# The first FFN token group moved into the last attention group of a gated cross-attention and FFN block

## The chip, the cores and the metric

The kernel runs on one core of a Trainium2 chip. The metric is the time of one execution on the device in microseconds, of which the median of several runs is taken. In the profile, PE is TensorE (PEld its weight loads), DVE is VectorE, ACT is ScalarE, POOL is GpSimd and SP is SyncE, whose queue issues all DMAs here.

## The reference

The input x has 16 sequences of 100 tokens with 512 features; the context has 361 tokens for each sequence. All is float32.

```
x = x + tanh(g_xattn) * attention(layernorm(x), ctx)     # RMS norm with weight, 16 heads of 32, masked softmax,
                                                         # out @ wo.T, times sigmoid(xnorm @ wg.T)
x = x + tanh(g_ffn) * ffn(layernorm(x))
ffn: gate, up = split(x @ w_gu)                          # w_gu: 512 x 2816, 4-bit codes, a scale for each 128 rows
     h = silu(gate) * up                                 # 1408 hidden features
     y = h @ w_down                                      # 1408 x 512, 4-bit codes, a scale for each 128 rows
     y / sqrt(mean(y*y) + 1e-6)
```

Products are made to float32 accuracy from a high and a low part of each operand.

## The kernel before, in words

**Attention.** The 16 sequences are taken in four groups of four (numbers 0 to 3 below). A group has 16 steps, one for each head. In a step PE turns the probabilities of head i (`transpose_probs`), ACT writes the high part of the turned tile (`probsT_hi`) and DVE the low part (`probsT_lo`); PE multiplies head i-1 with the values (`attend`) and DVE divides it (`attn_norm`). DVE takes the row maximum of head i+2 (`row_max`) and ACT its exponential (`exp_step`). Beside this each step has jobs from the hand-written table `BESIDE`: X (turned input), Q and K projections, A and B (values), G (gate product and tanh), T (turned attention output of four heads) and O (output product of one sequence, followed by `output` on DVE, which adds the residual). The steps run in a loop from step 6 to step 5 of the next group. The last group's steps 6 to 15 are written out; after them come `attend` of head 15, T3 and O0 to O3. The jobs of the steps 6 to 10 are G0; Q3, G1; K3; T1, G2; G3. T2 is in step 13. Only G, T and X jobs with a group to serve exist there.

Banks 2 to 5 of PSUM hold the scores of four heads, bank 6 the turned probabilities, bank 7 the attention product, banks 0 and 1 the jobs.

**FFN.** The 1600 tokens are taken in five token groups of 320; a group has 11 hidden tiles of 128 features. For a tile, `products` makes four gate products (one for each 128 input features) and four up products, each a pair of matmuls of 320 columns. The products go round five banks. ACT scales products 0 and 1 of each kind out of PSUM (`scale_product`), DVE adds products 2 and 3 (`scale_add`), POOL adds the two sums (`gate_sum`, `up_sum`), ACT takes tanh, DVE makes `gated` and `times_up`, ACT writes the high part of the hidden tile (`hidden_hi`) and POOL the low part (`hidden_lo`). The down products (`down`) of a group run beside the next group's tiles. The next group's LayerNorm is spread over the tiles: statistics at tiles 0 to 2, `ffn_normalise` at 3 to 5, the turning (`transpose_tile`, `mT_hi`, `mT_lo`) at 5, 7 and 9. The first group's LayerNorm stands in the last attention group, at steps 12 to 15; all its tiles come after the last attention output. Token group 0 holds tokens of attention group 0 only, token group 1 those of attention groups 0 and 1.

**Order.** Every engine runs its own list in order and waits on semaphores. SP's list has the outputs of attention group 2 at steps 2 to 5 of the last group, then the loads of the gate/up weights `wgu` (each behind the job that frees its memory), the group's rows of x1 (`xb`), all down weights `wdn`, the last outputs, and an increment of `s_stored`, for which ACT waits ahead of its first FFN instruction.

Lines of the kernel before that the steps below touch: 226 to 229 (the products' banks, `TURN_AT`), 289 (`STATS_AT`, `TURNED_AT`), 468 and 473 (loads of weights), 483 (load of x1), 671 to 684 (POOL), 880 to 894 (ACT), 1122 to 1148 and 1264 to 1279 (DVE), 1461 (turning), 1574 (products), 1587 (down).

## Time and profile before

| what | value |
|---|---|
| median of 3 runs | 663.53 us (663.25 to 663.76) |
| time of the profiled execution | 666.67 us |
| span of the profiled execution | 664.8 us |
| busy: PE, DVE, ACT, POOL | 589.5, 472.1, 323.3, 223.2 us |
| mean granted TensorE clock | 0.931 of full speed |

A clock of 1.00 in a row is 2.4 GHz, one of 0.50 is 1.2 GHz, and a value between is a stretch with both. Steps 6 to 15 of the last attention group run from 328.4 to about 374 us, the outputs to 390, token group 0 of the FFN from there to 440, and the other four groups to the end.

### The profile page before, as it was taken

Reading aid. Unit: us, or ns where it says so; the run is one execution under the profiler, and the core shown is the slowest. Engines: PE = TensorE matmul, PEld = TensorE weight load, DVE = VectorE, ACT = ScalarE, POOL = GpSimd, SP = SyncE. Lnnn points to the kernel's source line nnn. Section 1 sums busy time; section 2 is a strip of 40 time slices with the busy share of each in tenths; the row PEclk is TensorE's granted clock in tenths of the full one; section 3 lists DMA queues with packets and bytes.
Section 4 is the critical chain, followed back from the end, with each engine's and each line's share of the span. In section 5 each row is a group of like instructions: output and inputs, shape, how many; then the busy total and the mean of one; then the engine's idle time right before and its main releaser. Section 6 shows DMA issues by size and latency. Waiting matters only on the chain.

```text
span 664.8 us, 12492 instructions
## 1 busy us (share of the span) xinstructions
PE 589.5 (89%) x4154; PEld 516.5 (78%) x4154; DVE 472.1 (71%) x1062; ACT 323.3 (49%) x865; POOL 223.2 (34%) x242
## 2 busy tenths in 40 slices
PE   1689998999989899899996776899999998999996
PEld 0678878978779788797885555777798897799984
DVE  6745786867968579686635339989889889877631
ACT  2554454533454334453444115665675665666620
POOL 5630111000120001200000006676686666686640
PEclk9977997989999799878997599899999999999999
DMA  7460033531336222312377330200210020011011
GB/s 263 158 174 3 34 124 100 180 98 50 102 136 188 80 70 70 120 62 104 112 296 272 133 113 0 72 1 0 72 34 5 28 95 10 32 33 33 26 43 43
DMA packets 26841, 59.36 MB, mean 89 GB/s; under 512 B 3624, under 2 KB 3752, under 8 KB 26792
## 3 DMA queue, kind: packets, MB, share of 16 engines
q1 hardware_dynamic: 26792, 58.76, 26.8%
q8 instruction: 24, 0.39, 0.3%
q14 instruction: 25, 0.20, 0.1%
HBM read 39.62 MB, written 19.14 MB: 88 GB/s over the span
## 4 chain that ended last, share of the span: by engine, by line
PE 50%; DVE 23%; issue 10%; ACT 7%; POOL 7%; DMA 2%; DVEq 0%; SPq 0%; ACTq 0%; POOLq 0%
PE bank L257 20%; PE bank L1574 11%; PE bank L1587 10%; PE bank L1422 3%; POOL hT_lo L671 2%; DVE part_gate L1264 2%; PE bank L1398 2%; DVE vb_lo L947 2%; ACT probs L761 2%; DVE pT_lo L984 2%; DVE nmax L979 2%; DVE xn L974 2%; POOL ctxT_lo L603 2%; DVE hidden L1279 1%; POOL part_gate L678 1%
## 5 line engine op out<-in xcount | busy, mean ns | idle before, releaser
L1574 PE MATMUL bank<-mT_hi,wgu 128*128 128x320 f32 x440 | 140.2, 329 | 19.9 <-DVE part_up L1264 8.4
L1574 PE MATMUL bank<-mT_lo,wgu 128*128 128x320 f32 x440 | 133.7, 314 | 0.0
L761 ACT ACTIVATE probs<-bank,nmax 100x96 f32<-100x96 f32 x256 | 66.3, 343 | 128.1 <-DVE nmax L979 128.1
L1574 PEld LDWEIGHTS bank<-mT_hi,wgu 128*128 128x128 f32 x440 | 84.4, 192 | 35.5 <-DVE part_up L1264 12.0
L1574 PEld LDWEIGHTS bank<-mT_lo,wgu 128*128 128x128 f32 x440 | 84.8, 193 | 3.2
L678 POOL TENSOR_TENSOR part_gate<-part_gate 128x320 f32<-128x320 f32 x55 | 57.2, 1040 | 74.2 <-DVE part_gate L1264 74.2
L880 ACT ACTIVATE part_up<-bank,scale 128x320 f32<-128x320 f32 x110 | 57.2, 522 | 50.7 <-PE bank L1574 50.7
L1264 DVE SCALAR_TENSOR_TENSOR part_up<-bank,scale,part_up 128x320 f32<-128x320 f32 x110 | 58.4, 545 | 18.8 <-ACT part_up L880 18.1
L880 ACT ACTIVATE part_gate<-bank,scale 128x320 f32<-128x320 f32 x110 | 52.1, 526 | 35.3 <-SPq L560 19.2
L608 POOL TENSOR_TENSOR rstd<-var,halfpow 100x1 f32<-100x1 f32 x16 | 9.1, 567 | 173.9 <-DVE var L969 173.9
L684 POOL TENSOR_TENSOR part_up<-part_up 128x320 f32<-128x320 f32 x55 | 57.1, 1038 | 25.5 <-DVE part_up L1264 23.5
L1264 DVE SCALAR_TENSOR_TENSOR part_gate<-bank,scale,part_gate 128x320 f32<-128x320 f32 x110 | 55.2, 542 | 13.4 <-ACT part_gate L880 12.7
L1587 PE MATMUL bank<-wdn_lo,hT_hi 128*128 128x512 f32 (+1 forms) x143 | 56.4, 394 | 0.0
L1587 PE MATMUL bank<-wdn_hi,hT_hi 128*128 128x512 f32 (+1 forms) x143 | 56.1, 393 | 0.0
L1587 PE MATMUL bank<-wdn_hi,hT_lo 128*128 128x512 f32 (+1 forms) x143 | 55.8, 390 | 0.0
L1422 PE MATMUL bank<-vb_hi,pT_hi 128*100 128x68 f32 x192 | 51.4, 268 | 0.1
L1422 PE MATMUL bank<-vb_lo,pT_hi 128*100 128x68 f32 x192 | 51.3, 267 | 0.0
L1422 PE MATMUL bank<-vb_hi,pT_lo 128*100 128x68 f32 x192 | 51.3, 267 | 0.0
L671 POOL TENSOR_TENSOR hT_lo<-hidden,hT_hi 128x320 fp32r<-128x320 f32 x55 | 49.4, 898 | 4.6 <-ACT hT_hi L894 3.9
L984 DVE TENSOR_TENSOR pT_lo<-bank,pT_hi 128x300 fp32r<-128x300 f32 x64 | 29.8, 466 | 18.0 <-ACT pT_hi L769 17.3
L979 DVE TENSOR_REDUCE nmax<-bank 100x4 f32<-100x384 f32 x64 | 35.0, 549 | 4.8 <-PE bank L1398 4.8
L947 DVE TENSOR_TENSOR vb_lo<-bank,vb_hi 32x256 fp32r<-32x256 f32 (+2 forms) x56 | 23.6, 422 | 19.3 <-ACT vb_hi L741 14.3
(130 smaller groups left out, 1566.8 us busy)
## 6 DMA issues: line engine op xcount, KB each, us to landing
gate_up_scratch<-left SPq DMA_DIRECT2D x12, 512.0 KB, 6.1
down_scratch<-left SPq DMA_DIRECT2D x12, 512.0 KB, 3.2
wgu<-gate_up_scratch SPq DMA_DIRECT2D x11, 512.0 KB, 7.2
words<-in_packed SPq DMA_DIRECT2D x18, 256.0 KB
xn<-in_x SPq DMA_DIRECT2D x16, 200.0 KB
xa<-in_x SPq DMA_DIRECT2D x16, 200.0 KB
x_scratch<-gate SPq DMA_DIRECT2D x16, 200.0 KB
ctx_raw<-in_ctx_tail SPq DMA_DIRECT2D x4, 768.0 KB, 8.4
```

What stands on the lines that cost most here:

```text
L257: last = nc.tensor.matmul(out_ap, lhs(a, t), rhs(b, t), start=t == 0 and p == 0, stop=t == tiles - 1 and p == 2)
L671: nc.gpsimd.tensor_tensor(hT[LO][:, t, cols], hidden[n % 2][:, :], hT[HI][:, t, cols].bitcast(F32), ALU.subtract)\
L678: nc.gpsimd.tensor_tensor(a[:, :], a[:, :], b[:, :], ALU.add).then_inc(s_gate_sum, 1)
L684: nc.gpsimd.tensor_tensor(a[:, :], a[:, :], b[:, :], ALU.add).then_inc(s_up_sum, 1)
L761: last = nc.scalar.activation(probs[i % 2][:, cols], SC[i % HPG][0:L, cols], ACT.Exp, bias=nmax[:, i % 4, b:b + 1])
L880: nc.scalar.activation(part[n % 2][i][k][:, :], product_bank(j, t, i, k)[:, 0:TG], ACT.Copy, scale=scale32[:, t, i, k:k + 1]).then_inc(s_e ...
L979: nc.vector.tensor_reduce(nmax[:, i % 4, :], SC[i % HPG][0:L, 0:KC].rearrange("t (b k) -> t b k", b=NB), AXIS_X, ALU.max, negate=True).the ...
L984: nc.vector.tensor_tensor(pT[i % 2][LO][:, :, :].rearrange("k c t -> k (c t)"), PT[:, 0:CHUNKS * L], pT[i % 2][HI][:, :, :].rearrange("k c ...
L1264: nc.vector.scalar_tensor_tensor(onto, product_bank(j, t, i, k)[:, 0:TG], scale32[:, t, i, k:k + 1], onto, ALU.mult, ALU.add).then_inc(s_e ...
L1422: last = nc.tensor.matmul(PV[0:L, VW * c:VW * c + 2 * VW].rearrange("t (b w) -> t b w", w=VW), pT[i % 2][ph][:, c, :], vb[vh][:, c, :, VW ...
L1574: last = nc.tensor.matmul(product_bank(j, t, i, k)[:, 0:TG], wgu[t][:, k, 128 * i:128 * i + 128], mT[j % 2][half][:, k, :], start=half == ...
L1587: last = nc.tensor.matmul(bank[6 + slot][0:rows, :], hT[a][:, c, cols], wdn[c][b][:, :], start=c == 0 and p == 0, stop=c == FT - 1 and p == 2)
```

## The change

Token group 0 of the FFN is computed beside the last attention group. Its statistics are taken in step 6, its three row tiles are normalised in steps 7, 8, 9 and turned in steps 8, 9, 10. Its hidden tiles 0 to 4 follow one a step in steps 11 to 15; then come `attend` of head 15 ("H"), tile 5, T3, tile 6, O0, O1, tile 7, O2, O3, and tiles 8 to 10. Token group 1's statistics move to tiles 2 to 4, its normalising to 5 to 7, its turning to 7 to 9. The first two tiles use the product banks 0, 2 and 3, the next six also bank 4, and from then on there are five. Jobs G2 and G3 use bank 0 and O0 to O3 banks 1 and 5 in turn. SBUF is laid out anew so that these tiles find memory; the loads are issued in another order, the down weights with a semaphore for each tile. `ffn_tile` on each engine holds what the loop over tiles held before, in the same order within a tile.

```diff
-        ROUND, TURNED = (5, 2, 0, 3, 4), bank[1]
-        TURN_AT = (5, 7, 9)
+        STATS_AT, NORMED_AT, TURNED_AT = 6, {7: 0, 8: 1, 9: 2}, {8: 0, 9: 1, 10: 2}
+        FIRST_AT = {11: 0, 12: 1, 13: 2, 14: 3, 15: 4}
+        AT_LAST = ("H", 5, "T3", 6, "O0", "O1", 7, "O2", "O3", 8, 9, 10)
+
+        STATS_BESIDE, NORM_BESIDE, TURN_BESIDE = (0, 1, 2), (3, 4, 5), (5, 7, 9)
+        STATS_BESIDE_0, NORM_BESIDE_0, TURN_BESIDE_0 = (2, 3, 4), (5, 6, 7), (7, 8, 9)
+        def turned(j, m):
+            return bank[(6, 7, 1)[m]] if j == 1 else bank[1]
+        def banks_of(n):
+            return (0, 2, 3) if n < 2 else (0, 2, 3, 4) if n < 8 else (0, 2, 3, 4, 5)
+        for n in range(FT * FGROUPS):
+            for p in range(2 * KT):
+                number = min(banks_of(n), key=lambda m: left_at.get(m, (-1, m)))
+                PRODUCT_BANK[n, p], BEFORE[n, p] = number, left_at.get(number)
+                left_at[number] = (n, p)
-        STATS_AT, TURNED_AT = 12, {13: 0, 14: 1, 15: 2}
-        BANK_OF_LAST = {**BANK_OF, **dict(O0=0, O1=1, O2=3, O3=4)}
+        BANK_OF_LAST = {**BANK_OF, **dict(G2=0, G3=0, T2=1, T3=1, O0=1, O1=5, O2=1, O3=5)}
 # SP, in step 13 of the last loop cycle (attention group 2)
+                    elif i == CONTEXT_AT:
+                        sp.wait_ge(s_pj, split_count(GROUPS - 1, "X3"))
+                        for b in range(NB):
+                            sp.wait_ge(s_x1st[b], 32)
+                        load_x1(0)
 # SP, after the last cycle
-                sp.wait_ge(s_ctxlo, KT * GROUPS)
-                sp.wait_ge(s_pj, split_count(GROUPS - 1, "X3"))
-                load_gate_up((5, 6))
                 sp.wait_ge(s_pj, split_count(GROUPS - 1, "B2"))
-                load_gate_up((0, 1, 2, 3, 4))
+                load_gate_up(range(0, 4))
+                sp.wait_ge(s_pj, split_count(GROUPS - 1, "Q3"))
+                load_gate_up(range(4, 5))
                 sp.wait_ge(s_pj, split_count(GROUPS - 1, "K3"))
-                load_gate_up((7, 8, 9, 10))
+                load_gate_up(range(5, FT))
+                load_down(range(0, 1))
+                for b in range(NB):
+                    sp.wait_ge(s_x1st[b], 48)
+                next_x1(1)
                 sp.wait_ge(s_g, NB * GROUPS)
-                for b in range(NB):
-                    sp.wait_ge(s_x1st[b], 32)
-                load_x1(0)
-                load_down()
+                sp.wait_ge(s_sc, STEPS * GROUPS)
+                load_down(range(1, 2))
                 for b in range(NB):
                     output(GROUPS - 1, b, True)
+                    if b == 1:
+                        for other in range(NB):
+                            sp.wait_ge(s_x1st[other], 64)
+                        next_x1(2)
+                load_down(range(2, 10))
                 for b in range(NB):
                     sp.wait_ge(s_x1st[b], 16 * (GROUPS + 1))
-            sp.sem_inc(s_stored, 1)
+                sp.sem_inc(s_stored, 1)
+                load_down(range(10, FT))
 # ACT, DVE and PE, at the end of a step of the last group
+                if last and i in FIRST_AT:
+                    ffn_tile(0, FIRST_AT[i])
 # PE: what a product waits for where no product had its bank before
+                elif PRODUCT_BANK[n, p] == 5:
+                    pe.wait_ge(s_gated, NB * GROUPS)
+                elif beside_attention and PRODUCT_BANK[n, p] == 0:
+                    pe.wait_ge(s_gate, NB * GROUPS)
+                elif beside_attention:
+                    pe.wait_ge(s_exp, STEPS * GROUPS - HPG + PRODUCT_BANK[n, p] - 1)
 # PE, after step 15 (DVE and ACT alike, with their own parts)
-                attend(GROUPS - 1, STEPS - 1)
-                pe.wait_ge(s_mtlo, 3)
-                job(GROUPS, "T3")
-                for b in range(NB):
-                    job(GROUPS, f"O{b}")
+                for part_of in AT_LAST:
+                    if part_of == "H":
+                        attend(GROUPS - 1, STEPS - 1)
+                    elif isinstance(part_of, int):
+                        ffn_tile(0, part_of, True)
+                    else:
+                        job(GROUPS, part_of)
-            for j in range(FGROUPS):
+            for j in range(1, FGROUPS):
                 for t in range(FT):
...
```

POOL's list has the same FFN work as before; it does not name the attention's last steps.

## Rows read from the trace of the kernel before

**Rows 1.** Busy time by stage: stretch, its length, then each engine's busy time.
```profile
core 0: us, PE busy (x) PEld busy (x) DVE busy (x) ACT busy (x) POOL busy (x), PEclk, DMA share, GB/s
328.40:352.40 24.00, 24.00 (x244) 20.45 (x243) 9.32 (x25) 10.35 (x33) 0.00 (x0) 1.00 0.70 259
352.40:374.10 21.70, 12.48 (x85) 11.32 (x84) 13.64 (x43) 7.14 (x22) 0.88 (x1) 0.64 0.84 297
374.10:390.15 16.05, 14.73 (x52) 10.30 (x53) 4.90 (x7) 0.50 (x1) 0.00 (x0) 0.75 0.19 54
390.15:440.20 50.05, 37.76 (x188) 30.59 (x186) 39.80 (x85) 28.57 (x65) 29.10 (x30) 0.90 0.15 45
440.20:640.00 199.80, 192.14 (x1088) 171.16 (x1088) 168.25 (x366) 127.26 (x297) 141.96 (x149) 1.00 0.10 31
```

**Rows 2.** Waits from 395 to 430 us: us in total, times, longest.
```profile
ACT part_gate L880 <- SPq L560: 19.2, 1, 19.2
```

**Rows 3.** The chain of waits: start, duration, what.
```profile
349.44 2.93 PE bank L257 x12
...
368.04 1.11 PE bank L1461 x4
...
376.32 14.01 PE bank L257 x48
...
391.93 2.50 DMA x_scratch<-gate
```

**Rows 4.** Timeline of DVE, steps 11 to 13: start, duration, instruction, idle before it.
```profile
353.35 0.47 DVE L984 TENSOR_TENSOR pT_lo<-bank,pT_hi 128x300 fp32r<-128x300 f32 x1 [3.33 <-ACT pT_hi L769]
...
354.15 0.55 DVE L979 TENSOR_REDUCE nmax<-bank 100x4 f32<-100x384 f32 x1
356.11 0.47 DVE L984 TENSOR_TENSOR pT_lo<-bank,pT_hi 128x300 fp32r<-128x300 f32 x1 [1.42 <-ACT pT_hi L769]
...
357.38 1.86 DVE L1122 BATCH_NORM_STATS2 stats<-xb 128x6 f32<-128x512 f32 x3
...
360.90 1.17 DVE L1140 TENSOR_SCALAR mn<-xb,mv,rstd 128x128 f32<-128x128 f32 x4 [1.00 <-POOL rstd L647]
```

**Rows 5.** Timeline of ACT: one step's exponentials, one scaled product.
```profile
354.73 1.04 ACT L761 ACTIVATE probs<-bank,nmax 100x96 f32<-100x96 f32 x4 [1.42 <-DVE nmax L979]
...
403.01 0.51 ACT L880 ACTIVATE part_up<-bank,scale 128x320 f32<-128x320 f32 x1
```

**Rows 6.** Timeline of DVE: an attention output, then token group 0.
```profile
391.15 0.75 DVE L1005 SCALAR_TENSOR_TENSOR gate<-gate,coef_a,xa 100x512 f32<-100x512 f32 x1
...
401.19 1.00 DVE L1264 SCALAR_TENSOR_TENSOR part_gate<-bank,scale,part_gate 128x320 f32<-128x320 f32 x2
...
404.49 1.00 DVE L1264 SCALAR_TENSOR_TENSOR part_gate<-bank,scale,part_gate 128x320 f32<-128x320 f32 x2
...
410.16 1.07 DVE L1279 TENSOR_TENSOR hidden<-hidden,part_up 128x320 f32<-128x320 f32 x1 [0.75 <-POOL part_up L684]
...
418.84 0.99 DVE L1264 SCALAR_TENSOR_TENSOR part_gate<-bank,scale,part_gate 128x320 f32<-128x320 f32 x2
419.76 0.49 DVE L1279 TENSOR_TENSOR hidden<-hidden,part_up 128x320 f32<-128x320 f32 x1
420.16 2.29 DVE L1140 TENSOR_SCALAR mn<-xb,mv,rstd 64x128 f32<-64x128 f32 x4
...
442.88 1.01 DVE L1264 SCALAR_TENSOR_TENSOR part_gate<-bank,scale,part_gate 128x320 f32<-128x320 f32 x2
```

**Rows 7.** Timeline of PE: one product, a pair of matmuls.
```profile
430.14 0.42 PE L1574 MATMUL bank<-mT_hi,wgu 128*128 128x320 f32 x1 [0.40 <-ACT part_up L880]
430.39 0.31 PE L1574 MATMUL bank<-mT_lo,wgu 128*128 128x320 f32 x1
```

**Rows 8.** SP's queue: first and last of 22 down-weight issues.
```profile
353.41 0.58 SPq L473 DMA_DIRECT2D wdn_hi<-down_scratch  x1
...
364.29 0.43 SPq L473 DMA_DIRECT2D wdn_lo<-down_scratch  x1
```

More of the change, by code:

```diff
@@ L203, in build @@
         s_unit = sem("gate_up_scales_cast")
[L204 removed]
+        s_wgu, s_wdn = [sem(f"gate_up_weight{t}") for t in range(FT)], [sem(f"down_weight{c}") for c in range(FT)]
         s_xb = sem("x1_loaded")
@@ L856, in _ @@
                     mT_hi(0, m)
+                act.wait_ge(s_unit, 1)
+                for t in range(FT):
+                    ffn_tile(0, t)
             with act.Else():
@@ new lines, in ffn_tile @@
+            def ffn_tile(j, t):
+                for n in tiles_done(j, t):
+                    mean_square(n)
+                for k in (2, 3):
+                    scale_add(j, t, 0, k)
+                if t:
+                    times_up(j, t - 1)
+                elif j:
+                    times_up(j - 1, FT - 1)
+                for m in beside_tile(j, t, STATS_BESIDE_0, STATS_BESIDE):
+                    ffn_stats(j + 1, m)
+                for m in beside_tile(j, t, NORM_BESIDE_0, NORM_BESIDE):
+                    ffn_normalise(j + 1, m)
+                for k in (2, 3):
+                    scale_add(j, t, 1, k)
+                gated(j, t)
+                for n in tiles_done(j, t):
+                    output_tile(n)
+                for m in beside_tile(j, t, TURN_BESIDE_0, TURN_BESIDE):
+                    mT_lo(j + 1, m)
@@ L1236, in _ @@
                     mT_lo(0, m)
+                for t in range(FT):
+                    ffn_tile(0, t)
             with dve.Else():
@@ L1319, in _ @@
+            for j in range(1, FGROUPS):
+                for t in range(FT):
+                    ffn_tile(j, t)
             for n in tiles_done(FGROUPS, 0):
@@ L1497, in full_job, with products, down, ffn_tile @@
                 last.then_inc(f_pj, 1)
+            def products(j, t, i, beside_attention):
+                if t == 0 and i == 0:
+                    pe.wait_ge(s_mtlo, 3 * j + 3)
+                if j == 0 and i == 0:
+                    pe.wait_ge(s_wgu[t], 16)
+                for k in range(KT):
+                    open_bank_of(FT * j + t, KT * i + k, beside_attention)
+                    for half in (HI, LO):
+                        last = nc.tensor.matmul(product_bank(j, t, i, k)[:, 0:TG], wgu[t][:, k, 128 * i:128 * i + 128], mT[j % 2][half][:, k, :],
+                                                start=half == HI, stop=half == LO)
+                    last.then_inc(s_gu, 1)
+            def down(n, c):
+                rows, slot = OTILES[n], n % 2
+                cols = ring(128 * n, rows)
+                if c == 0 and n >= 2:
+                    pe.wait_ge(s_yo, n - 1)
+                if n == 0:
+                    pe.wait_ge(s_wdn[c], 32)
+                pe.wait_ge(s_hlo, FT * ((128 * n + rows - 1) // TG) + c + 1)
+                for p, (a, b) in enumerate(PASSES):
+                    last = nc.tensor.matmul(bank[6 + slot][0:rows, :], hT[c][a][:, cols], wdn[c][b][:, :],
+                                            start=c == 0 and p == 0, stop=c == FT - 1 and p == 2)
+                last.then_inc(s_dn, 1)
+            def ffn_tile(j, t, beside_attention=False):
+                for m in beside_tile(j, t, TURN_BESIDE_0, TURN_BESIDE):
+                    if (j, m) == (0, 2):
+                        pe.wait_ge(s_gated, NB * GROUPS)
+                    transpose_tile(j + 1, m)
+                chunks = chunks_beside(j, t)
+                products(j, t, 0, beside_attention)
+                for n, c in chunks[:1]:
+                    down(n, c)
+                products(j, t, 1, beside_attention)
+                for n, c in chunks[1:]:
+                    down(n, c)
             with pe.If(wants_full(pe)):
@@ L1537, in _ @@
                     transpose_tile(0, m)
+                for t in range(FT):
+                    ffn_tile(0, t)
             with pe.Else():
@@ L1578, in down @@
-            def down(n, c):
-                rows, slot = OTILES[n], n % 2
-                cols = ring(128 * n, rows)
-                if c == 0 and n >= 2:
-                    pe.wait_ge(s_yo, n - 1)
-                if n == 0 and c == 0:
-                    pe.wait_ge(s_wdn, 16 * 2 * FT)
-                pe.wait_ge(s_hlo, FT * ((128 * n + rows - 1) // TG) + c + 1)
-                for p, (a, b) in enumerate(PASSES):
-                    last = nc.tensor.matmul(bank[6 + slot][0:rows, :], hT[a][:, c, cols], wdn[c][b][:, :],
-                                            start=c == 0 and p == 0, stop=c == FT - 1 and p == 2)
-                last.then_inc(s_dn, 1)
@@ L1603, in _ @@
+            for j in range(1, FGROUPS):
+                for t in range(FT):
+                    ffn_tile(j, t)
             for n in TILES_BESIDE[FGROUPS]:
```

400 lines of the change are left out of this document (204 added, 196 removed).

## The prediction

> **What bounds the kernel now.** I read four views: the busy time by stage, the waits, the chain of waits, and the timeline of each engine where the change works.
>
> By stage [rows 1], PE is busy for all 24.00 us of the steps 6 to 10 at a clock of 1.00, while DVE has 9.32 and ACT 10.35 us of work: PE sets that stage, and the chain runs through its jobs (349.44, a job of 12 matmuls of 512 columns, 2.93 us) [rows 3]. From 352.4 on nobody is full. In the steps 11 to 15 PE has 12.48 us of 21.70, at a clock of 0.64; from 374 to 390 the four output products hold PE, with DVE at 4.90 of 16.05; and token group 0 of the FFN lasts 50.05 us with PE at 37.76, DVE at 39.80, ACT at 28.57 and POOL at 29.10. These are 88 us in which each engine has work for 42 to 65. Token group 0's hidden tiles depend on x rows that were finished three attention groups earlier, so the two idle stages can be laid over each other. In the four groups behind 440.2 PE is at 192.14 of 199.80 us; the change does not touch their work.
>
> I measure by two DVE instructions that both kernels have. `pT_lo` of step 11 starts at 353.35 [rows 4]; the first `scale_add` of group 1's tile 0 starts at 442.88 [rows 6]. Between them lie 89.5 us.
>
> **Steps 6 to 10: +1.5 us.** Statistics (1.86 us) and their POOL power, then three normalisings (1.17 us each while POOL is idle) [rows 4], go into steps 6, 7, 8 and 9. With three `mT_lo` (about 0.6, by the 300-column 0.47 of `pT_lo`) that is about 7.5 us more on a DVE that idles 14.7 us there [rows 1], so most is hidden. PE is the full engine: its three turnings took 1.11 us for four transposes at a clock of 0.50 [rows 1, 3]; at 1.00 I take half, and for the third (64 rows) a quarter, 1.3 us together. Step 8's normalising and `mT_lo` also stand ahead of `pT_lo` of step 9, so that the maximum and exponential of head 11 are 1.7 us late, but the scores that need their bank come only behind T1, G2 and a turning on PE, which covers all but 0.2 us. Bounds: 1.1 (turnings alone) and 4 (the 2.9 us of one job's cover gone as well). The load of x1 now sits in step 13 of the loop cycle before; its waits are for things long done. ACT's new wait for the kept weight pieces is met by the time it comes.
>
> **Steps 11 to 15: 28.5 us where there were 21.** Each step now has a tile behind its attention work on every engine. For tiles 0 and 1 there are three banks, so product 3 waits for ACT's first scaling, and ACT comes to it only behind the exponential. Link by link from the start of one `pT_lo` to the next: `pT_lo` 0.39 and `attn_norm` 0.41 (starts 353.35 to 354.15), maximum 0.55, exponentials 0.05 + 1.04, scaling of product 0 0.53, hand-over and product 3 0.10 + 0.56 (430.14 to the end of the pair at 430.70), `scale_add` 0.54, POOL's gate sum 0.26 + 1.05, tanh 0.5, `gated` 0.5, together 6.35 [rows 4, 5, 6, 7] (POOL: 29.10 us in 30, and the full sums are slightly longer than that mean [rows 1]). The same stretch took 2.76 us before (353.35 to 356.11). Step 13 has four banks, but T2 and a statistic as well: 6.7. In steps 14 and 15 maximum and exponential are gone and DVE's own work sets the pace: attention 0.8, scaled sums 2 x 0.93, `times_up` 0.4, `gated` 0.4, a statistic 0.6 = 4.05, and with aggregation, variance and the last division 5.05. Sum 6.35 + 6.35 + 6.7 + 4.05 + 5.05 = 28.5. Nothing hides these links. Bounds: 5 x 4.05 = 20 if no link waits, and 5 x 8 = 40 if tanh and products of each tile are paid in full behind exponentials.
>
> **Tiles 5 to 10 with the outputs: 34.2 us.** In group 0 before, plain tiles came every 3.30 us (401.19 to 404.49) [rows 6], which is POOL's three operations; a tile with a normalising took 4.8, because the normalising beside POOL takes 2.29 us and not 1.17 (418.84: sums, `times_up` 0.40, 2.29) [rows 4, 6]. Now: tile 5 4.8; T3 0.5; tile 6 4.8; O0 and O1 3.9; tile 7 with normalising and `mT_lo` 5.6; O2 and O3 3.7; tile 8 3.9; tile 9 3.7; tile 10 3.3. The output figures: two jobs cost PE 5.6 to 5.9 us [rows 3], DVE 2 x 1.47 (0.72 + 0.75) [rows 6]; PE finishes tile 6's products 1.2 us into DVE's tile, so the jobs run under the rest of it and DVE waits about 1 us. Total 34.2 by DVE. PE for itself needs 6 x 2.35 for products and some 14 for outputs, transposes and turnings, 28 us at 1.00, so it is not the bound.
>
> **What goes away** within the 89.5: ACT's first FFN instruction waited 19.2 us for `s_stored` behind the last stores (2.50 us of DMA in the chain) [rows 2, 3]. Now ACT meets that wait ahead of group 1. SP has 16 weight issues ahead of it; 22 took 11.4 us [rows 8], so 16 take 8.2, and tiles 8 to 10 (10.9 us) cover them with some 2 us to spare. The same 4 MB of `wdn` at the 297 GB/s of the second stage [rows 1] land in 14 us, and group 1 asks for two a tile from 12 us on: just hidden. The loads of `wgu` begin behind the same output of attention group 2 as before, in step 5, and the first tile asks for its weights in step 11, 24 us and more later [rows 1].
>
> **Clock: +4 us.** With about 3.6 us of matmuls (at 1.00) in a step of 6.3, PE is 56% busy. The rows have 0.64 for a stage with about a third of its time in full-clock work, and 0.90 for group 0 [rows 1]. I take half the time at 1.2 GHz in steps 11 to 15, where each such step costs 1.1 us more (transposes, and two or three products on the chain, 0.15 a matmul), 2.5 us; and 1.5 in the outputs (48 matmuls took 14.01 us at 0.75 against 4 x 2.93) [rows 1, 3]. Bounds 0 and 11. The Trainium skill ("TensorE: Matmul & The Clock Gate", What's actually happening) has it that the throttled state is the default and activity releases it. The trace agrees, 0.64 in the thin stage and 1.00 behind 440 us. By that rule alone the filled steps would run at 1.00 and the 4 us would be 0.
>
> **POOL beside attention outputs: +1 us.** DVE's `times_up`, with both inputs in SBUF, took 1.07 us beside POOL at 410.16 and 0.49 at 419.76 [rows 6]. The four residual additions (L1005, 0.75) had an idle POOL and now have a busy one. Bounds 0 and 4 x 1.05. The Trainium skill ("SBUF — State Buffer", Who interferes with whom) says that a DVE instruction with two SBUF inputs waits out a GpSimd instruction that reads SBUF, as one lock. Row 410.16 agrees; each addition held for a whole POOL instruction would give the upper bound.
>
> **Sum.** 1.5 + 28.5 + 34.2 + 4 + 1 = 69.2 us in place of 89.5: -20.3. The profiled execution of 666.67 us becomes 646.4. The median of the runs, 663.53, is 3.1 us below it; with the same difference it becomes **643.2 us**.
>
> **The rivals.**
>
> *Longer steps (B).* Handshakes between four in-order lists seldom meet as well as on paper. For it: DVE waited 3.33 us for ACT at 353.35 and 1.42 at 356.11 with hardly any other work [rows 4]. Against: most of 6.35 us is already waits. At 8 us a step in place of 5.7, +11.5: 654.7.
>
> *Outputs and tiles at 1.2 GHz (C).* For it: PE's clock was 0.64 and 0.75 in the two stages before 390 [rows 1]. Products 25.6, outputs 4 x 5.6 = 22.4, rest 4 and waits 2, 54 in place of 34.2 + 1.5: +18, 661. Against: PE is over 80% filled there at full clock.
>
> *The second half of SP's list (D).* `s_stored` or `wdn` come late, at 220 GB/s or with slower issues: ACT or `down` waits 2 to 6 us at group 1's start: 647. For it: only 2 us of margin.
>
> *All meets well (E).* Clock 1.00 and four-bank steps at 5: 643.2 - 4 - 3.5 = 636.
>
> *Slower than before (F).* A step of 11 to 15 pays the attention's round (2.76 us) and a tile's whole passage, product to `up_sum`, one behind the other. The passage alone is 7 us: product 0.6, scaling and sums 1.6, POOL's gate and up sum 2.6, tanh, `gated` and `times_up` 1.5, hand-overs 0.7 [rows 5 to 7]; with a statistic and a division 10.7 us a step, 53.5 for five: +25 on the forecast's 28.5, 668. It decides from 5.7 + 20.3 / 5 = 9.8 us a step. Against it: in group 0 successive tiles overlapped down to 3.30 us.
>
> *It does not do what it says (G).* If a wait on a late bank or load kept tiles 0 to 4 out of the steps, they would follow them: about as before, 662. The waits of products are for `s_exp`, `s_gate` and `s_gated`, each done by the time that the tile's turn comes, so this is unlikely.
>
> **How the numbers follow.** Forecast (637 to 649) 0.55, B 0.18, C 0.05, D 0.09, E 0.07, F 0.03, G 0.03. The range leaves out E's better half, and C, F and G: 636 to 655. Faster by over 0.2% (1.3 us, about what a measurement tells from none): all but F and part of G, 0.95; within 0.2% 0.02, slower 0.03.
>
> **What would show it.** Right: DVE from `pT_lo` of step 11 to group 1's first `scale_add` in about 69 us; step 11 starts 1 to 2 us later; `pT_lo` starts 6 to 7 us apart in steps 11 to 13 and 4 to 5 behind them; ACT's wait for `s_stored` gone or under 1 us; the stretch behind it as long as before (222 us). Wrong: steps of 8 us or more (B, F), a clock under 0.8 in the output stage (C), a wait of PE for a DMA or of ACT for SP at group 1's first tile (D), more than 3 us gained or lost behind it.

## The result, and the profile after

The changed kernel takes 647.24 us in the median of 4 runs (640.88 to 651.23), beside 663.64 us for the kernel before; the ratio is 0.9711, 95% interval 0.9632 to 0.9791. Forecast were 643.2 us and 636 to 655. The profiled execution is the 651.23 us one, the longest of the four and left out of the ratio; its span is 649.4 us beside 664.8. Where its extra time sits turned out to be the main finding, so it is kept as the trace of after.

I cut both traces at four instructions that both kernels have, all on DVE: `pT_lo` of the first step of the first group, `pT_lo` of steps 6 and 11 of the last group, and the first `scale_add` of FFN group 1.

| stretch, us | before | after | difference | forecast |
|---|---|---|---|---|
| start to first `pT_lo` | 47.13 | 53.00 | +5.87 | 0 |
| to step 6 of the last group | 282.48 | 282.34 | -0.14 | 0 |
| steps 6 to 10 | 23.74 | 25.24 | +1.50 | +1.5 |
| step 11 to group 1's first `scale_add` | 89.53 | 65.93 | -23.60 | -21.8 |
| from there to the end | 221.92 | 222.89 | +0.97 | 0 |

So steps 6 to 10 and the rebuilt stretch together give 22.1 us, 1.8 more than forecast, and the profiled execution gets 15.4 of them. Of the rest, 5.9 us go at the start, in code whose work the change does not touch, and 1.0 behind group 1's first `scale_add`.

By stage, after: steps 6 to 10, steps 11 to 15, tiles 5 to 10 with the outputs, in the columns of [rows 1].
```profile
335.34:360.58 25.24, 25.01 (x252) 21.15 (x244) 15.11 (x47) 11.56 (x35) 0.88 (x1) 1.00 0.74 270
360.58:390.34 29.76, 25.09 (x154) 21.99 (x154) 22.30 (x59) 18.69 (x48) 13.37 (x14) 0.89 0.11 34
390.34:426.51 36.17, 32.66 (x161) 26.36 (x160) 31.30 (x62) 17.17 (x40) 17.81 (x20) 0.91 0.45 148
```
The two thin stages of before (PE 12.48 of 21.70 and DVE 4.90 of 16.05) are gone: PE is busy for 84% and 90% of the two new ones, and the clock stands at 0.89 and 0.91 where it stood at 0.64 and 0.75.

The waits of ACT from 395 to 430 us after, in total, times, longest. The 19.2 us for `s_stored` [rows 2] has no row left; what heads the list is the two spells in which PE makes outputs:
```profile
ACT part_gate L919 <- PE bank L1622: 11.7, 3, 6.0
ACT part_up L919 <- PE bank L1622: 3.6, 5, 1.7
ACT hT_hi L933 <- DVE hidden L1286: 2.9, 4, 1.8
```
The chain through those spells, after (start, duration, what) [rows 3]: 48 output matmuls in 11.03 us where they took 14.01.
```profile
394.83 3.52 PE bank L1622 x12
398.35 5.52 PE bank L314 x24
403.87 0.44 PE bank L1570 x4
404.31 2.68 PE bank L1622 x16
406.99 5.51 PE bank L314 x24
```
DVE's timeline after, step 11 and the start of step 12 (start, duration, instruction, idle before it) [rows 4, 6]: the attention's three instructions, the maximum, then the tile's two pairs of sums, each behind ACT or PE.
```profile
360.58 0.47 DVE L1078 TENSOR_TENSOR pT_lo<-bank,pT_hi 128x300 fp32r<-128x300 f32 x1
...
361.38 0.55 DVE L1073 TENSOR_REDUCE nmax<-bank 100x4 f32<-100x384 f32 x1
363.65 1.01 DVE L1271 SCALAR_TENSOR_TENSOR part_gate<-bank,scale,part_gate 128x320 f32<-128x320 f32 x2 [1.72 <-PE bank L1622]
365.79 1.08 DVE L1271 SCALAR_TENSOR_TENSOR part_up<-bank,scale,part_up 128x320 f32<-128x320 f32 x2 [1.13 <-ACT part_up L919]
366.79 0.48 DVE L1279 SCALAR_TENSOR_TENSOR hidden<-tgate,part_gate 128x320 f32<-128x320 f32 x1
367.27 0.47 DVE L1078 TENSOR_TENSOR pT_lo<-bank,pT_hi 128x300 fp32r<-128x300 f32 x1
```
ACT's work in that step [rows 5]: the exponentials and product 0's scaling lie one behind the other, as the link list had it.
```profile
361.96 1.03 ACT L839 ACTIVATE probs<-bank,nmax 100x96 f32<-100x96 f32 x4 [1.42 <-DVE nmax L1073]
362.87 0.96 ACT L919 ACTIVATE part_gate<-bank,scale 128x320 f32<-128x320 f32 x2
```
DVE's timeline after among the outputs [rows 6]: tiles 5, 6, 7, 8 and group 1 begin at the `part_gate` rows; O0 and O1 stand between 401.20 and 405.37.
```profile
390.34 1.00 DVE L1271 SCALAR_TENSOR_TENSOR part_gate<-bank,scale,part_gate 128x320 f32<-128x320 f32 x2
391.66 1.07 DVE L1286 TENSOR_TENSOR hidden<-hidden,part_up 128x320 f32<-128x320 f32 x1 [0.32 <-POOL part_up L736]
...
396.04 0.99 DVE L1271 SCALAR_TENSOR_TENSOR part_gate<-bank,scale,part_gate 128x320 f32<-128x320 f32 x2
...
401.20 0.69 DVE L1095 SCALAR_TENSOR_TENSOR gate<-gate,bank 100x512 f32<-100x512 f32 x1 [0.29 <-PE bank L314]
401.92 0.75 DVE L1099 SCALAR_TENSOR_TENSOR gate<-gate,coef_a,xa 100x512 f32<-100x512 f32 x1
403.98 0.69 DVE L1095 SCALAR_TENSOR_TENSOR gate<-gate,bank 100x512 f32<-100x512 f32 x1 [1.30 <-PE bank L314]
...
405.37 1.00 DVE L1271 SCALAR_TENSOR_TENSOR part_gate<-bank,scale,part_gate 128x320 f32<-128x320 f32 x2
...
414.70 1.01 DVE L1271 SCALAR_TENSOR_TENSOR part_gate<-bank,scale,part_gate 128x320 f32<-128x320 f32 x2 [0.63 <-ACT part_gate L919]
...
417.91 1.07 DVE L1279 SCALAR_TENSOR_TENSOR hidden<-tgate,part_gate 128x320 f32<-128x320 f32 x1 [0.22 <-ACT tgate L925]
...
426.51 1.00 DVE L1271 SCALAR_TENSOR_TENSOR part_gate<-bank,scale,part_gate 128x320 f32<-128x320 f32 x2
```
SP's queue after [rows 8], the first and last of 18 down-weight issues. They end 2.5 us ahead of group 1's first `scale_add`.
```profile
414.44 0.36 SPq L528 DMA_DIRECT2D wdn_hi<-down_scratch  x1
...
423.62 0.43 SPq L528 DMA_DIRECT2D wdn_lo<-down_scratch  x1
```
Now the start, which no group of before covers. PE's timeline, first the kernel before, then after: both have a wait behind the branch that chooses between the full-mask code (never taken with this input) and the common code; only after has a second one, inside the first scores. "<-issue" says that the engine waited for nothing that the profile records.
```profile
37.06 0.37 PE L1391 MATMUL bank<-mb,ones 1*100 1x384 bf16 x4 [3.31 <-issue]
```
```profile
36.56 0.56 PE L1495 MATMUL bank<-mb,ones 1*100 1x384 bf16 x4 [3.06 <-issue]
...
37.64 0.40 PE L1502 MATMUL bank<-kT_hi,qT_lo 32*100 32x96 f32 x4
44.04 0.41 PE L1502 MATMUL bank<-kT_hi,qT_hi 32*100 32x96 f32 x4 [6.00 <-issue]
```
The loads there, after, from 39 to 43 us (queue: packets, MB, share of the 16 DMA engines): what SP issued behind its own branch fills them (x rows and context of the next attention group, code words, scales), and two packets of a kind "instruction" run in the same stretch.
```profile
q1 hardware_dynamic: 437, 1.09, 95.9%
q8 instruction: 1, 0.02, 1.8%
q14 instruction: 1, 0.01, 0.9%
```

### The profile page after: what moved, and what is told of

The parts are those of the page before. It is cut to its first block, busy times and chain, and to the rows that moved or that the text cites. A ratio compares the mean times of both kernels' runs of the same rounds, so it can differ in the third digit from the quotient of the medians.

```text
span 649.4 us, 12494 instructions
## 1 busy us (share of the span) xinstructions
PE 582.3 (90%) x4154; PEld 511.7 (79%) x4154; DVE 474.4 (73%) x1062; ACT 322.8 (50%) x865; POOL 223.6 (34%) x242
## 4 chain that ended last, share of the span: by engine, by line
PE 51%; DVE 21%; issue 10%; POOL 8%; ACT 8%; DMA 1%; DVEq 0%; POOLq 0%; ACTq 0%; SPq 0%
PE bank L314 19%; PE bank L1622 14%; PE bank L1635 10%; PE bank L1526 3%; ACT probs L839 2%; PE bank L1502 2%; POOL ctxT_lo L673 2%; DVE vb_lo L1041 2%; POOL hT_lo L723 2%; DVE part_gate L1271 2%; DVE nmax L1073 2%; DVE pT_lo L1078 2%; DVE xn L1068 2%; DVE hidden L1286 1%; PE bank L1513 1%
## 5 line engine op out<-in xcount | busy, mean ns | idle before, releaser
L736 POOL TENSOR_TENSOR part_up<-part_up 128x320 f32<-128x320 f32 x55 | 57.0, 1037 | 23.8 <-DVE part_up L1271 22.1
L1041 DVE TENSOR_TENSOR vb_lo<-bank,vb_hi 32x256 fp32r<-32x256 f32 (+2 forms) x56 | 23.6, 422 | 16.4 <-ACT vb_hi L819 15.0
```

What stands on the lines that cost most here:

```text
L736: nc.gpsimd.tensor_tensor(a[:, :], a[:, :], b[:, :], ALU.add).then_inc(s_up_sum, 1)
```

## The experiments

Two questions: what the parts of the gain are, and what the 5.9 us at the start are. The theory for the second (called the fetch theory here): PE fetches its code in blocks; a branch over longer code moves the running code against the block boundaries, and a boundary now lies in the first scores, where SP's first burst of loads has the DMA engines full. Each run below was compared with runs of the kernel before on the same chip, in three groups: the first four (the kernel before: 664.95 us), the next four on another chip (664.99), and the three with idle instructions (665.85). Medians of different groups are best compared by their ratios.

In these runs' traces, one execution each (us; "first" is the first `pT_lo`, "waits" PE's "<-issue" waits at the start, "stretch" step 11 to group 1, 89.53 before and 65.93 after):

| kernel | first | waits | stretch | median (range, runs) | ratio to before, 95% |
|---|---|---|---|---|---|
| short other path | 45.90 | 1.75 | 65.95 | 644.03 (642.51-644.6, 5) | 0.968, 0.9659-0.9701 |
| before, long other path | 49.06 | 2.01 + 2.41 | 89.58 | 668.14 (665.0-670.99, 8) | 1.0045, 1.0021-1.0068 |
| tiles behind the steps | 49.85 | 1.84 + 4.11 | 69.58 | 651.79 (650.6-656.37, 6) | 0.9814, 0.9787-0.9842 |
| outputs apart | 51.14 | 1.58 + 5.25 | 74.32 | 657.45 (655.65-658.04, 6) | 0.9879, 0.986-0.9899 |
| common path first | 43.47 | none | 71.94 | 647.5 (646.19-649.24, 5) | 0.9743, 0.9724-0.9763 |
| late loads | 48.48 | 2.13 + 2.19 | 66.10 | 646.21 (644.91-648.58, 5) | 0.9721, 0.9699-0.9743 |
| fourth bank for tile 1 | 51.01 | 3.33 + 3.93 | 65.85 | 647.8 (644.82-651.72, 6) | 0.9737, 0.9706-0.9768 |
| outputs one by one | 51.47 | 3.54 + 5.04 | 66.33 | 648.22 (643.97-651.66, 6) | 0.9736, 0.9708-0.9764 |
| 80 idle instructions | 46.54 | 2.99 | 66.04 | 643.37 (639.42-645.53, 6) | 0.9671, 0.9629-0.9713 |
| 20 idle instructions | 54.01 | 3.47 + 6.41 | 65.85 | 649.36 (648.1-652.2, 4) | 0.9767, 0.9717-0.9817 |
| 80 idle and late loads | 46.15 | 2.40 | 65.95 | 642.7 (640.63-643.92, 6) | 0.9669, 0.963-0.9708 |

**Short other path.** The change gives the full-mask path group 0's eleven tiles too, a second copy of their code ahead of the common one. This kernel leaves them out there; that code is not run.
```diff
             with pe.If(wants_full(pe)):
...
-                for t in range(FT):
-                    ffn_tile(0, t)
             with pe.Else():
```
(the same two lines on ACT, DVE and POOL)

> The changed kernel with the eleven FFN tiles left out of the other branch (the path for full masks, which these inputs never take; that path alone is cut short). Nothing that runs is changed, only how much code lies ahead of the branch that runs. Theory A (the changed kernel loses some 6 us at its start because TensorE waits for its own code behind the branch, and how long depends on where the code lies): TensorE's idle time without a releaser between 32 and 46 us falls from 9.1 us to 3 to 4, pT_lo of step 0 starts near 47.1 and not at 53.0, the median falls by about 6 us to 641. Theory B (the new SBUF layout or the order of loads delays the start): no change, 647, first pT_lo at 53. Theory C (chance from run to run): the first pT_lo is spread in both kernels, medians equal within 2 us.

Measured: the second wait is gone, the first `pT_lo` comes at 45.90 in place of 53.00, the stretch is as after, and the median is 644.03; 641 was expected, from the profiled execution of the changed kernel, which lies 4 us above its median. Taking away code that never runs wins 2.1 us by the ratios (0.968 beside 0.9711) and 3.2 by the medians. The four runs of the changed kernel are too few to tell this from none: their interval, 0.9632 to 0.9791, covers it. Two kernels further down ("fourth bank", "outputs one by one") have the second wait at the same place and nearly the same stretch, and their intervals begin at 0.9706 and 0.9708, above this one's end at 0.9701.

**The kernel before with a longer other path.** The reverse, on the kernel that has nothing of the change: 176 matmuls, each with its weight load (352 instructions), in PE's never-taken path.
```diff
                 for m in range(3):
                     transpose_tile(0, m)
+                for n in range(11):
+                    for p in range(8):
+                        for half in (HI, LO):
+                            nc.tensor.matmul(FJ[:, 0:TG], wgu[n][...], mT[0][half][:, p % 4, :], ...)
```


> The kernel before with 176 matmuls more in TensorE's other branch, which does not run. Theory A: the start is delayed although nothing that runs has changed; if the same place of the code is hit, by about 6 us (669), else by another amount within 0 to 8 us, shown as idle time without a releaser on TensorE between 32 and 46 us (3.3 us before). Theory B: 663.6, as before.

Measured: 3.2 us slower, at an interval that excludes 1. PE's timeline of this kernel has a second wait where before had none, but behind 47 matmuls of the first scores, not 28:
```profile
36.31 0.56 PE L1391 MATMUL bank<-mb,ones 1*100 1x384 bf16 x4 [2.01 <-issue]
...
38.22 0.40 PE L1398 MATMUL bank<-kT_lo,qT_hi 32*100 32x96 f32 x3
41.03 0.39 PE L1398 MATMUL bank<-kT_lo,qT_hi 32*100 32x96 f32 x1 [2.41 <-issue]
```
The place of the wait is what later gave the sharpest test.

**Tiles 0 to 4 behind the steps.** The same order of everything, but no tile beside a step.
```diff
-        FIRST_AT = {11: 0, 12: 1, 13: 2, 14: 3, 15: 4}
-        AT_LAST = ("H", 5, "T3", 6, "O0", "O1", 7, "O2", "O3", 8, 9, 10)
+        FIRST_AT = {}
+        AT_LAST = ("H", 0, 1, 2, 3, 4, 5, "T3", 6, "O0", "O1", 7, "O2", "O3", 8, 9, 10)
```


> The changed kernel with tiles 0 to 4 behind attend of head 15 and not in steps 11 to 15 (LayerNorm and turning stay in steps 6 to 10). My sum: steps 11 to 15 fall from 29.8 us (trace) to about 15 (five steps of 2.8 to 3 and T2), the five tiles then take 3.3 to 3.9 us each, 18; so +3 to +5 us, 651. Rival (the steps' idle time is what the change gains): the five tiles cost their full 4.3 us each and nothing comes back in the steps, +12 or more, 659. Rival 2: the tiles cost more in the steps than behind them, under 645.

Measured: the stretch grows by 3.65 us, the median by 4.6 (3 to 5 expected). DVE's timeline of this kernel: the attention's steps end early, and plain tiles follow at 3.30 us.
```profile
372.37 1.08 DVE L1272 SCALAR_TENSOR_TENSOR part_gate<-bank,scale,part_gate 128x320 f32<-128x320 f32 x2 [1.25 <-ACT part_gate L919]
...
379.11 1.01 DVE L1272 SCALAR_TENSOR_TENSOR part_gate<-bank,scale,part_gate 128x320 f32<-128x320 f32 x2
382.41 1.01 DVE L1272 SCALAR_TENSOR_TENSOR part_gate<-bank,scale,part_gate 128x320 f32<-128x320 f32 x2
```
So "a tile a step", the part that names the change, is worth 3.7 of the 23.6 us. This is also the case that the prediction priced as rival G, at 662 us: the tiles follow the steps and do not overlap them. It takes 651.79. In order the five steps and five tiles take 33.3 us, together 29.8: what a step leaves idle in the middle is given back as hand-overs.

**Outputs apart.** Tiles 5 to 10 behind all four outputs and not among them.
```diff
-        AT_LAST = ("H", 5, "T3", 6, "O0", "O1", 7, "O2", "O3", 8, 9, 10)
+        AT_LAST = ("H", "T3", "O0", "O1", "O2", "O3", 5, 6, 7, 8, 9, 10)
```


> The changed kernel with T3 and the four outputs together ahead of tiles 5 to 10, none between tiles. My sum: the outputs then cost their TensorE time of 11.7 us plus 2 us of waits for T3 and the first sum, where they cost DVE 8.4 us among the tiles (4.9 and 3.5 in the trace), so +4 to +6 us, 652. Rival (interleaving hides nothing, since DVE still waits for TensorE at O0 and O1): within 1 us of 647.

Measured: +8.4 us in the stretch, more than expected. DVE's timeline of this kernel shows both halves of the price: a wait of 5.67 us for the first output and of 1.3 to 1.5 for each next one.
```profile
396.12 0.69 DVE L1095 SCALAR_TENSOR_TENSOR gate<-gate,bank 100x512 f32<-100x512 f32 x1 [5.67 <-PE bank L314]
399.08 0.69 DVE L1095 SCALAR_TENSOR_TENSOR gate<-gate,bank 100x512 f32<-100x512 f32 x1 [1.49 <-PE bank L314]
...
406.02 1.00 DVE L1271 SCALAR_TENSOR_TENSOR part_gate<-bank,scale,part_gate 128x320 f32<-128x320 f32 x2
```
With the 3.7 this makes 12.1 of 23.6 us, if the two add up; no run has both. The other 11.5 are common to both experiments, and no run takes them apart. What both keep is that group 0's rows are turned early and that ACT's 19.2 us wait is gone: before, the first `scale_add` of group 0 came 4.3 us behind the start of the last residual addition, after a wait for ACT (DVE's timeline of the kernel before):
```profile
395.43 1.01 DVE L1264 SCALAR_TENSOR_TENSOR part_gate<-bank,scale,part_gate 128x320 f32<-128x320 f32 x2 [3.53 <-ACT part_gate L880]
```

**Common path first.** The branch's condition is inverted on every engine, so that the running code comes first and PE falls into it.
```diff
-            with pe.If(wants_full(pe)):
+            with pe.If(wants_common(pe)):
```


> The changed kernel with the two branches of every engine exchanged: the flag is inverted, so that the branch that runs follows directly on the start and its end jumps over the other one. The work is the same. Theory A (TensorE waits for code behind a taken branch): the idle time without a releaser at the start (9.1 us in the changed kernel's trace) goes, a similar but smaller wait of 2 to 4 us appears at the jump ahead of FFN group 1, net -3 to -7 us: 640 to 644. Theory B (the start is late for another reason): first pT_lo still near 53 us, 647.

Measured: a miss, 647.5 us where 640 to 644 were expected. There is no wait at the start any more, but PE now has to jump over the other path at the end of its own, and pays there, in the first products of group 1 (PE's timeline of this kernel):
```profile
417.70 0.60 PE L1622 MATMUL bank<-mT_hi,wgu 128*128 128x320 f32 x1 [4.93 <-issue]
```
The stretch is 6.0 us longer, 4.9 of it this row, and what lies behind it 1.7 (224.60 beside 222.89). The loop up to step 6 was 3.2 us shorter (279.15), which is not the order of the branches: 2.5 of it is one step of the first attention group, in which PE is busy throughout and which takes 3.33 us here and 5.83 in the changed kernel. It takes 3.33 at a clock of 1.00 in the traces of "tiles behind the steps" and "80 idle and late loads" too, and 5.83 at 0.63 after. So executions differ in where the clock stands, whatever the layout.

**Late loads.** SP holds the first burst of loads behind its branch (not FFN loads, but x rows and context of the next attention group, and code words) until the first scores are made.
```diff
             with sp.Else():
+                sp.wait_ge(s_sc, HPG)
```


> The changed kernel with SP's first loads behind its branch (residual, tokens and context of the next group, code words: some 2.4 MB) held until the first four score tiles are done. Theory A1 (the second wait of TensorE for code is long because that fetch shares the DMA engines with this burst): the second wait falls from 4 to 6 us to 1 to 2.5, the median by 2 to 4 us to 644, if the loads are still in time. Theory A2 (the fetch takes as long without the burst): the second wait stays at 4 to 6 us, median 647. In both, later loads could delay step 6, which would show as a longer stretch from the first pT_lo to the last group.

Measured: the second wait is 2.19 us, where it took 3.93 to 6.00 at this place in the five traces with the burst, so its length hangs on the loads and its being there does not. The median is 646.21, 1.0 us lower where 2 to 4 were expected; the intervals do not tell it from the changed kernel's.

**Two changes of the stretch itself.** A fourth bank for tile 1 already, and the outputs spread among the tiles one by one.
```diff
-            return (0, 2, 3) if n < 2 else (0, 2, 3, 4) if n < 8 else (0, 2, 3, 4, 5)
+            return (0, 2, 3) if n < 1 else (0, 2, 3, 4) if n < 8 else (0, 2, 3, 4, 5)
```


> The changed kernel with four banks and not three for tile 1 (bank 4 is free in step 12 once head 14's exponential is done). If product 3's wait for ACT's first scaling sets step 12 (my chain): step 12 falls from 7.1 us by about 0.7 us, since ACT's scaling itself still stands behind the exponential; median -0.5, not measurable beside 647. Rival (the number of banks sets the steps): -2 us or more in step 12.


```diff
-        AT_LAST = ("H", 5, "T3", 6, "O0", "O1", 7, "O2", "O3", 8, 9, 10)
+        AT_LAST = ("H", 5, "T3", 6, "O0", 7, "O1", "O2", 8, "O3", 9, 10)
...
-            return (0, 2, 3) if n < 2 else (0, 2, 3, 4) if n < 8 else (0, 2, 3, 4, 5)
+            return (0, 2, 3) if n < 2 else (0, 2, 3, 4) if n < 9 else (0, 2, 3, 4, 5)
```


> The changed kernel with one output job between tiles where it has two: 6, O0, 7, O1, O2, 8, O3, 9 (tile 8 then with four banks). DVE waited 2 us for TensorE at O0, O1 and O3; if single outputs are hidden under a tile's own DVE work, the stretch from pT_lo of step 11 to group 1 falls from 66 by 1 to 2 us, 645.5. Rival (down weights are issued behind O3 and come late at group 1): the gain is lost again at its tiles 1 to 4, 647 or more.

Measured: 65.85 and 66.33 us beside 65.93, so neither moves the stretch; both expectations missed. Outputs one by one were to gain 1 to 2 us. With the fourth bank step 12 was to fall by 0.7 us from 7.1, and it takes 7.73. Bank 4 had not been used for a product yet, so tile 1's first product is given it, and now that product stands behind head 14's exponential (PE's timeline of this kernel); after, it started right behind the attention's matmuls (367.73). What step 12 loses comes back between tiles 6 and 7, which are 8.68 us apart and not 9.33.
```profile
367.88 0.39 PE L1622 MATMUL bank<-mT_hi,wgu 128*128 128x320 f32 x1 [2.23 <-ACT probs L839]
```

**Idle instructions ahead of the common code.** If the boundary is the cause, it can be moved at will. 20 or 80 semaphore increments in PE's never-taken path change nothing that runs.
```diff
                 phase_barrier(pe)
+                for _ in range(80):
+                    pe.sem_inc(s_apart, 1)
```


> As the run with 80, with 20 idle semaphore increments in PE's code of the branch that is never taken. Theory A: the boundary comes 20 instructions earlier, so the second wait stands behind 18 or 19 matmuls of the first scores in place of 28, and costs 2 to 6 us as in the changed kernel; median 646 to 649. Rival (no fixed boundary): the second wait stays behind 28 matmuls, or goes elsewhere.

Measured: 649.36 us, just above the expected 646 to 649, and the second wait, 6.41 us, is now behind 4 + 12 + 2 = 18 matmuls, 10 fewer than 28, which with their weight loads are the 20 instructions that were added. It splits a row of four matmuls (PE's timeline of this kernel):
```profile
37.17 0.41 PE L1495 MATMUL bank<-mb,ones 1*100 1x384 bf16 x4 [3.47 <-issue]
...
37.72 0.42 PE L1502 MATMUL bank<-kT_hi,qT_hi 32*100 32x96 f32 x2
44.55 0.40 PE L1502 MATMUL bank<-kT_hi,qT_hi 32*100 32x96 f32 x2 [6.41 <-issue]
```


> The changed kernel with 80 idle semaphore increments put into PE's code of the branch that is never taken; nothing that runs is changed, only where the code of the taken branch lies. Two traces already say where the second wait falls: 28 matmuls (56 instructions with their weight loads) behind the branch in the changed kernel, 47 (94) in the kernel before with 352 instructions added, and the other branch's code is 35 instructions longer in the first (387 against 352): a boundary every 256 instructions fits both (38 against 35). Theory A (PE has to fetch the next block of code at a fixed boundary, and 5.9 us were lost because that boundary lies in the first scores): 80 instructions move it from 56 to about 232 instructions behind the branch, where nothing waits for it, as in the kernel before; one wait of 1.7 to 3.5 us behind the branch, no second one, the first pT_lo at 44 to 48 us in place of 53.0, median 643 to 645, and a spread of 2 to 4 us in place of 10. Rival (the length of the skipped code is what counts, or the start merely scatters): two waits as before, first pT_lo at 49 to 54, median 647 to 648.

Measured: one wait, none in the scores, the stretch as after, 643.37 us. PE's timeline of this kernel, from the branch past the scores without a gap:
```profile
36.48 0.57 PE L1495 MATMUL bank<-mb,ones 1*100 1x384 bf16 x4 [2.99 <-issue]
36.55 0.57 PE L1502 MATMUL bank<-kT_hi,qT_hi 32*100 32x96 f32 x4
...
38.56 0.40 PE L1502 MATMUL bank<-kT_hi,qT_lo 32*100 32x96 f32 x4
38.89 0.58 PE L314 MATMUL bank<-wv_hi,ctxT_hi 128*128 128x256 f32 x1
```
The two kernels ran on the same chip and differ in 60 instructions that are never executed; their intervals, 0.9629 to 0.9713 and 0.9717 to 0.9817, do not meet. The expected spread of 2 to 4 us was not met: it is 6.1 us, and the one with 20, which has the second wait, spreads by 4.1. So these spreads do not follow the wait. In every kernel here the shortest run has the highest mean granted clock or one within 0.005 of it: 640.88 us at 0.956 and 651.23 at 0.938 for the changed kernel, 659.96 at 0.941 and 666.68 at 0.931 for the kernel before.

With the loads held as well, so that the wait behind the branch has the DMA engines to itself:

> The run with 80 increments, and SP's first burst of FFN loads held until the first scores of step 0 are there, so that what PE fetches behind the branch has the DMA queues to itself. Theory A: the one wait left falls from 1.7 to 3.5 us towards 1.5 to 2.1 (2.13 us was what remained of it with the loads held and two waits), median 642 to 644.5, at most 1 us better than with the 80 alone. Rival (the wait behind the branch does not depend on the loads): same median as with the 80 alone within 0.5 us, or slower where the held loads come late.

Measured: that wait is 2.40 us, the median 642.7 and the ratio 0.9669, the lowest of all, though not told apart from the 80 instructions alone. From 34 to 36.4 us the only traffic is three packets of the kind "instruction" (packets, MB, share):
```profile
q14 instruction: 3, 0.02, 3.3%
```
So the loads are not what makes the wait behind the branch (1.5 to 2.1 us had been expected), and holding them adds nothing that can be told once the boundary is out of the way. Both kernels with 80 instructions lie below the kernel before, and below the changed kernel by its median; against the one with 20 the difference is clear of the intervals.

## Why the prediction was right, and where it was not

The time was inside the range, and the stages that were described came out as described. Two things should be set against that. It was luck that the range was wide enough for a cost that no term of it covered (5.87 us at the start), of which about 1 us each was offset by steps 11 to 15 and by residual additions that cost nothing more. And the overlap of tiles with steps, which the prediction is built around, carries only 3.7 us of the gain. Step by step:

- **Steps 6 to 10, +1.5.** Measured +1.50. DVE had 6.7 us more work there (15.11 beside 8.37 between the same two instructions; 7.5 forecast), hidden beside a PE that is busy for 25.01 of 25.24 us.
- **Steps 11 to 15, 28.5 us by links.** `pT_lo` starts 6.69, 7.08, 6.79 and 4.08 us apart (360.58, 367.27, 374.35, 381.14, 385.22), and tile 5 begins 5.12 behind the last; forecast were 6.35, 6.35, 6.7, 4.05 and 5.05. Sum 29.76, with the clock's forecast 2.5 it was to be 31. The links listed for one step add up to 6.48 us and not to 6.35, which is nearer still. Walking one step's links by rows of before was good to 0.7 us a step. Rivals B and F (8 and 10.7 us a step) fall. G falls too, and its price was wrong by 10 us (662 beside the 651.79 of tiles behind the steps).
- **Tiles 5 to 10 with the outputs, 34.2 us, and the clock's 1.5.** 36.17. The groups: tile 5 to 6 5.70 (5.3 with T3), tile 6 and two outputs 9.33 (8.7), tile 7 and two outputs 9.33 (9.3), tiles 8 to 10 4.80, 3.72 and 3.29 (3.9, 3.7, 3.3). Tile 8 is the one that was mis-sized: it has two waits for ACT, of 0.56 us ahead of its second `part_up` and 0.22 ahead of `gated`, and `gated` takes 1.07 us beside POOL's `up_sum` (417.91) where it takes 0.49 in tile 9. What the forecast calls work for 42 to 65 us on each engine in the thin stages is 30 on POOL and 36 on ACT by [rows 1]; that only leaves more room.
- **The clock, +4 over both.** It stood at 0.89 and 0.91, so rival C (1.2 GHz through the outputs) falls; what was lost cannot be cut out of the links. Both stretches together came out 0.8 us below the sum with the clock (65.93 beside 66.7) and 3.2 above the sum without it. The "about 69 us" named as the sign for this stretch counts the 1.5 us of steps 6 to 10 in; by the prediction's own terms it is 67.7.
- **POOL beside the residual additions, +1.** The cost did not come, because its premise failed and not because such a collision is free: POOL was not busy at any of the four additions (401.92, 404.70, 411.50, 413.32). Its instructions end at 401.65 and 411.00 and begin again at 406.45 and 415.79. Each addition took 0.75 us, as before. `times_up` beside POOL did take 1.07 at 391.66, as the row at 410.16 had it.
- **SP's list.** The 16 issues ahead of `s_stored` took 8.6 us (414.44 to 423.04), 8.2 forecast, and ACT reaches group 1 at 425.84, 2.8 us later, where 2 were forecast. ACT's wait is gone. Rival D falls.
- **Behind group 1's first `scale_add`,** 222.89 beside 221.92: about as said.
- **The step that was missing.** The prediction went through every stage that the change touches and took the start for untouched. It touches one thing there: the never-taken path is written ahead of the common one, and the eleven tiles copied into it push the running code of PE on by 389 instructions (188 matmuls with their loads, and 13 waits by the built program; the expectation above has 387). In the profiled execution that is +5.87 us. How much of the median it is: the two layouts without the second wait, the loads as they are, give 643.4 and 644.0 beside 647.24 (ratios 0.9671 and 0.968 beside 0.9711), so 2 to 4 us. These medians mix runs at different clocks. Of the runs at a mean granted clock of 0.940 to 0.945 alone, the same two average 644.3 and 643.9, and the four layouts with the second wait beside the burst and the stretch as after (the changed kernel, here one run, the fourth bank, outputs one by one, 20 idle instructions) 648.3, 649.1, 649.6 and 650.3, so 4 to 6 us. By the ratios the kernel without the wait would run at 641.7 to 642.3 on the base of the forecast, about 1 us below the 643.2 that was forecast.

That the wait is tied to the code's position is shown (28, 47 and 18 matmuls for 389, 352 and 409 instructions; none at 469, none at 0), and that loads lengthen it (2.19 us with them held, 3.93 to 6.00 at the same place without). What PE waits for, the profile does not name. The traces' packets do, nearly: each second wait ends 1.2 to 1.4 us behind the landing of one 16 KB packet of the kind "instruction" on queue q8, in all eight traces that have such a wait. After, it is this packet, the only one of its queue from 41 to 42 us (packets, MB, share):
```profile
q8 instruction: 1, 0.02, 7.3%
```

| kernel, us | packet starts | lands | PE goes on |
|---|---|---|---|
| 20 idle instructions | 41.93 | 43.12 | 44.55 |
| after | 41.45 | 42.62 | 44.04 |
| outputs one by one | 41.09 | 42.33 | 43.58 |
| outputs apart | 39.84 | 40.98 | 42.20 |
| fourth bank for tile 1 | 38.61 | 40.91 | 42.29 |
| tiles behind the steps | 37.99 | 40.33 | 41.72 |
| before, long other path | 37.56 | 39.75 | 41.03 |
| late loads | 37.28 | 38.52 | 39.74 |

The wait right behind the branch ends 1.5 to 1.7 us behind such a packet in the twelve traces that jump there. In the four of them without a second wait the next one lands while PE still has work. What the burst lengthens can be seen too: three 8 KB packets of the same kind (queue q14) stand ahead of the 16 KB one, and the four start 2.25, 1.33 and 1.18 us apart after, 0.84, 0.51 and 0.44 with the loads held. So the fetch theory holds as far as a trace can show it. The Trainium skill ("Runtime: NRT & Kernel Launch", Instruction fetch mechanics) says that code comes in blocks of 256 instructions (16 KiB), prefetched in sequence, and that a taken branch out of the window waits for its page. The packets of 16 KB agree, and so do the positions: 37 instructions more put the wait 38 earlier, 20 more put it 20 earlier, and 80 more moved it out of the scores. The Trainium skill calls the crossing of a boundary mostly hidden there; with at most 2.3 us of work between a taken branch and the boundary it cost 2.2 to 6.4 us here.

## What to carry to other kernels

Code that never runs has a price if it lies ahead of code that does: after a change that lengthens one arm of a branch, look at the "<-issue" waits behind the branch, not only at the stages that were edited. To size work laid over other work, walk one round's links with durations from rows and take the hand-overs as paid; here that came within 1.3 us over five rounds, the clock aside. Then undo the parts one at a time: the overlap that gave the change its name was worth 3.7 us, putting tiles among the outputs 8.4 us, and 11.5 of the 23.6 us stay unassigned. Where runs of one kernel scatter by 10 us, compare them at the same mean granted clock before reading a difference of 2 to 4 us from medians.

## What the runs showed of the hardware that was not expected

- Behind PE's taken branch there was a wait of 1.6 to 3.5 us in every layout that jumps, 2.40 us even when three "instruction" packets were all that moved. With the common path first it went to the end of that path: 4.93 us.
- A second wait, 56 instructions (28 matmuls with their loads) behind the branch, took 3.93 to 6.00 us beside SP's burst and 2.19 us with it held. In one execution each it took 6.41 us 36 instructions behind the branch and, in the kernel before, 2.41 us 94 behind it. With 80 idle instructions there was none.
- PE went on 1.2 to 1.4 us behind the landing of a 16 KB "instruction" packet at each of the eight second waits.
- Idle instructions that are never executed, 80 of them, gave 643.37 us where 20 of them gave 649.36 on the same chip.
- The same step of the loop, with PE busy throughout, took 3.33 us in some executions (clock 1.00) and 5.83 in others (0.63).
